# Second attention: subtraction of the maximum on GpSimd, fields paired five apart, three pairs in flight

## The reference

```
cols = _unfold(y, WS, STRIDE, PAD)            # WS 8, STRIDE 6, PAD 3
attn = jnp.einsum('blhic,blhjc->blhij', q, k) + bias[None, None]
e = jnp.exp(attn - jnp.max(attn, axis=-1, keepdims=True))
s = jnp.sum(e, axis=-1, keepdims=True)
s_img = _reverse(s, H, W)                     # overlapping windows are added up
o = jnp.einsum('blhij,blhjc->blhic', e, v)
o_img = _reverse(o, H, W).reshape(B, HEADS, ch, H, W)
out = (o_img / s_img[:, :, None]).reshape(B, C, H, W)
out = _hft(_conv1x1(out, proj_w, proj_b), hft_w, hft_b)
```

## Time and profile before

| what | us |
|---|---|
| time, median of 3 runs | 5556.05 |
| lowest, highest | 5555.84, 5556.2 |
| the profiled execution: its time | 5562.28 |
| the profiled execution: its span | 5560.1 |
| second attention in it, first DMA to last store issued | 2513.2 to 3004.6 |

### The profile page before, as it was taken

The page is one execution under the profiler, slowest core; times in us unless marked ns, Lnnn a source line. Parts: engine busy times, 40 slices in busy tenths (PEclk is TensorE's granted clock), DMA queues, the critical chain, the costliest instruction groups (busy, mean ns, idle before and its releaser), DMA issues. The chain is left out here.

```text
span 5560.1 us, 84741 instructions
## 1 busy us (share of the span) xinstructions
PE 5052.6 (91%) x33796; PEld 2334.1 (42%) x33796; DVE 3792.1 (68%) x4563; ACT 2672.0 (48%) x3851; POOL 1419.3 (26%) x1156
## 2 busy tenths in 40 slices
PE   7799999999989998997886989999896999999989
PEld 2255555555544443445553433333332333333333
DVE  3476767767651112227987849998686999999953
ACT  1134444444442222324553135554475888888854
POOL 1000000000000001112223410000002999999930
PEclk9899999999989998998998999999997999999999
DMA  6521211112113122434443410000233475447454
GB/s 217 155 39 23 44 35 29 38 24 42 23 28 118 68 71 93 134 109 139 139 135 113 144 50 20 30 30 20 87 111 124 161 177 180 170 163 177 164 180 159
DMA packets 322564, 550.69 MB, mean 99 GB/s; under 512 B 147660, under 2 KB 283492, under 8 KB 318812
## 3 DMA queue, kind: packets, MB, share of 16 engines
q1 hardware_dynamic: 295900, 465.09, 28.1%
q0 software_dynamic: 15232, 63.76, 3.5%
q10 hardware_dynamic: 11040, 16.43, 1.0%
HBM read 379.09 MB, written 166.09 MB: 98 GB/s over the span
## 5 line engine op out<-in xcount | busy, mean ns | idle before, releaser
L3926 DVE TENSOR_TENSOR_SCAN s_h<-s_da,s_h 128x448 f32<-128x448 f32 x672 | 730.2, 1128 | 26.1 <-ACT s_da L3853 22.6
L3973 POOL TENSOR_TENSOR s_h<-s_dtu,s_bt 128x896 f32<-128x896 f32 x336 | 698.7, 2080 | 0.1
L3783 PE MATMUL s_py<-s_prod,s_idf 128*128 128x448 f32 x1344 | 573.9, 549 | 0.0
L623 PE MATMUL b_pc<-b_ca,b_wdm 128*113 128x392 f32 x1152 | 487.2, 520 | 31.3 <-DVE b_wdm L838 25.5
L766 ACT ACTIVATE b_band<-b_psel 124x784 f32<-124x784 f32 x264 | 217.4, 823 | 427.5 <-PE b_psel L691 424.4
L3853 ACT ACTIVATE s_da<-s_dt,s_al 128x448 f32<-128x448 f32 x672 | 401.9, 637 | 13.0 <-DVE s_h L3926 12.9
L623 PE MATMUL b_pc<-b_cb,b_wdm 128*113 128x392 f32 x960 | 402.0, 519 | 0.0
L1268 POOL MEMSET kept_f_wt<- 128x192 f32 x1 | 0.3, 257 | 1415.9 <-POOLq L144 1415.9
L3933 DVE TENSOR_TENSOR s_prod<-s_h,s_pc 128x896 f32<-128x896 f32 x336 | 356.8, 1062 | 1.4 <-issue 0.7
L2862 DVE SCALAR_TENSOR_TENSOR j_zc<-j_zt,kept_vec,j_zc 128x896 f32<-128x896 f32 x320 | 345.0, 1146 | 6.7 <-ACT j_zt L2804 6.4
L3783 PEld LDWEIGHTS s_py<-s_prod,s_idf 128*128 128x128 f32 x1344 | 246.4, 190 | 187.7 <-issue 167.0
(11 more groups left out here) (724 smaller groups left out, 10900.3 us busy)
## 6 DMA issues: line engine op xcount, KB each, us to landing
s_bt<-mid_brs SPq DMA_DIRECT2D x112, 896.0 KB, 4.4
s_bt<-mid_brs SPq DMA_DIRECT2D x112, 448.0 KB, 5.8
b_qk<-mid_qkvp SPq DMA_DIRECT2D x96, 240.2 KB
d_vt<-mid_vd SPq DMA_DIRECT2D x200, 96.0 KB
d_qs<-mid_qd SPq DMA_DIRECT2D x20, 744.0 KB, 5.7
d_ks<-mid_kd SPq DMA_DIRECT2D x20, 744.0 KB, 7.9
b_v<-mid_qkvp SPq DMA_DIRECT2D x6, 1922.0 KB
mid_pout<-d_out POOLq DMA_DIRECT2D x20, 558.0 KB, 4.3
```

The lines of the kernel that those rows point to most:

```text
L623: mm = pe.matmul(pc[n % 2][0:113, 0:392], wdm[:, slot, p, 0:113], src, start=(w == STARTS[a]), stop=(w + 1 == STARTS[a + 1]))
L3783: mm = pe.matmul(y, idf[:, :], prod[j % 3][:, e, :], start=(pr == 0 and e == 0), stop=False)
L3926: v.tensor_tensor_scan(x, along(da[m % 3][:, 0, 0:CH]), x, before_, ALU.mult, ALU.add).then_inc(scanned, 1)
L3973: p.tensor_tensor(h[j % HR][:, :, :], u, bt[t % BR][:, 2 * pr:2 * pr + 2, :], ALU.mult).then_inc(fed, 1)
```

## The change

Four things change together in `window_strips`.

1. The subtraction of the maximum leaves VectorE. GpSimd gets `shift(n)`, one instruction a pair over 768 elements.
2. A pair is fields i and i+5 instead of 2i and 2i+1. They don't overlap, so `lay(n)` is one instruction of 768 elements.
3. Three pairs are in flight: `d_sc` and `d_mx` are triple, PE, DVE and GpSimd run two pairs ahead (score(n+2), soft(n+2), shift(n+2)) where PE and DVE ran one ahead.
4. GpSimd's other work is cut up between the subtractions: one of the three window copies of the next strip at i = 0, 1 and 2, the clearing at i = 3. The store is issued by SyncE.

```diff
-        sc = [sb(f"d_sc{i}", [128, 2, 3 * 2 * 64]) for i in range(2)]
-        mx = [sb(f"d_mx{i}", [128, 12]) for i in range(2)]
+        sc = [sb(f"d_sc{i}", [128, 2, 3 * 2 * 64]) for i in range(3)]
+        mx = [sb(f"d_mx{i}", [128, 12]) for i in range(3)]
...
                 for k in range(2):
-                    x = STEP * (2 * i + k)
+                    x = STEP * (i + NP * k)
                     sp.dma_start(vt[n % NV][64 * k:64 * k + 64, :], vd[q, STEP * r:STEP * r + WS, x:x + WS, :]).then_inc(v_loaded[n % NV], 16)
...
                 if n + NV < NW:
                     values(n + NV)
+                if s >= 2 and i == 0:
+                    store(s - 2)
...
+            def shift(n):
+
+                p.wait_ge(max_found, n + 1)
+                p.tensor_tensor(group(n), group(n), mx[n % 3][:, :].rearrange("p (m o) -> p m o", o=1).broadcast_to([128, 12, 64]), ALU.subtract).then_inc(shifted, 1)
+
+            for t in range(3):
+                window(0, t)
             clear(0)
-            for s in range(NSTR):
-                if s + 1 < NSTR:
-                    window(s + 1)
+            shift(0)
+            shift(1)
+            for n in range(NW):
+                s, i = divmod(n, NP)
+                if n + 2 < NW:
+                    shift(n + 2)
+                if i == 0 and s % NR:
+                    carry(s)
+                if s + 1 < NSTR and i < 3:
+                    window(s + 1, i)
+                if s + 1 < NSTR and i == 3:
                     clear(s + 1)
-                if s:
-                    store(s - 1)
-                if (s + 1) % NR:
-                    carry(s + 1)
...
             score(0)
+            score(1)
             for n in range(NW):
                 s, i = divmod(n, NP)
-                if n + 1 < NW:
-                    score(n + 1)
+                if n + 2 < NW:
+                    score(n + 2)
                 turn(n)
...
             def soft(n):
-                o = n % 2
                 v.wait_ge(scored, n + 1)
-                if n >= 2:
-                    v.wait_ge(turned, n - 1)
-                v.tensor_tensor(sc[o][:, :, :], pS[:, :, 0:384], bt[:, :, :], ALU.add).then_inc(biased, 1)
+                if n >= 3:
+                    v.wait_ge(turned, n - 2)
+                v.tensor_tensor(sc[n % 3][:, :, :], pS[:, :, 0:384], bt[:, :, :], ALU.add).then_inc(biased, 1)
                 v.wait_ge(biased, n + 1)
-                by = sc[o][:, :, :].rearrange("p b (m j) -> p (b m) j", j=64)
-                v.tensor_reduce(mx[o][:, :], by, AX.X, ALU.max).then_inc(max_found, 1)
-                v.wait_ge(max_found, n + 1)
-                v.tensor_tensor(by, by, mx[o][:, :].rearrange("p (m o) -> p m o", o=1).broadcast_to([128, 12, 64]), ALU.subtract).then_inc(shifted, 1)
+                v.tensor_reduce(mx[n % 3][:, :], group(n), AX.X, ALU.max).then_inc(max_found, 1)
...
-                for k in range(2):
-                    x = STEP * (2 * i + k)
-                    dst = acc[s % 2][:, :, :, x:x + WS]
-                    if 2 * n + k:
-                        v.wait_ge(laid, 2 * n + k)
-                    v.tensor_tensor(dst, dst, pO[:, k, 0:384].rearrange("p (a h w) -> p a h w", a=6, h=WS), ALU.add).then_inc(laid, 1)
+                if n:
+                    v.wait_ge(laid, n)
+                dst = pair(acc[s % 2][:, :, :, STEP * i:STEP * i + WS])
+                v.tensor_tensor(dst, dst, pO[:, :, 0:384].rearrange("p k (a h w) -> p k a h w", a=6, h=WS), ALU.add).then_inc(laid, 1)
```

More of the change, by code:

```diff
@@ L1992, in window_strips @@
         lo, hi = slice(0, 64), slice(64, 128)
+        group = lambda n: sc[n % 3][:, :, :].rearrange("p b (m j) -> p (b m) j", j=64)
         def windows(t):
@@ L1997, in windows, with pair @@
             return bass.AP(tensor=a.tensor, offset=a.offset, ap=[list(a.ap[0]), [STEP, NR], [PW, WS], [1, WS]])
+        def pair(t):
+            a = t.copy()
+            return bass.AP(tensor=a.tensor, offset=a.offset, ap=[list(a.ap[0]), [STEP * NP, 2]] + [list(x) for x in a.ap[1:]])
         @block.sync
@@ L2016, in values, with store @@
                 for k in range(2):
-                    x = STEP * (2 * i + k)
+                    x = STEP * (i + NP * k)
                     sp.dma_start(vt[n % NV][64 * k:64 * k + 64, :], vd[q, STEP * r:STEP * r + WS, x:x + WS, :]).then_inc(v_loaded[n % NV], 16)
+            def store(s):
+                q, r = divmod(s, NR)
+                sp.wait_ge(p_evac, 3 * (s + 1))
+                sp.dma_start(rows(pout)[q, :, :, ON * r:ON * r + ON], out[s % 2][:, :, :]).then_inc(stored[s % 2], 16)
             strips(0)
@@ L2033, in _, with window @@
                     values(n + NV)
+                if s >= 2 and i == 0:
+                    store(s - 2)
+            store(NSTR - 2)
+            store(NSTR - 1)
+            sp.wait_ge(stored[0], 16 * NR)
+            sp.wait_ge(stored[1], 16 * NR)
         @block.gpsimd
         def _(p):
-            def window(s):
+            def window(s, t):
                 p.wait_ge(q_loaded[s % 2], 16 * (s // 2 + 1))
@@ L2040, in window @@
                     p.wait_ge(scored, NP * (s - 1))
-                for t in range(3):
-                    p.tensor_copy(qw[s % 2][:, t, :, :].rearrange("p n (h w) -> p n h w", w=WS), windows(qs[s % 2][:, t, :])).then_inc(windowed, 1)
+                p.tensor_copy(qw[s % 2][:, t, :, :].rearrange("p n (h w) -> p n h w", w=WS), windows(qs[s % 2][:, t, :])).then_inc(windowed, 1)
             def clear(s):
@@ L2051, in carry @@
             def carry(s):
-                p.wait_ge(laid, 2 * NP * s)
+                p.wait_ge(laid, NP * s)
                 p.tensor_copy(acc[s % 2][:, :, 0:2, :], acc[(s - 1) % 2][:, :, STEP:WS, :]).then_inc(acc_ready, 1)
[L2056 to L2061, removed]
-            clear(0)
-            for s in range(NSTR):
-                if s + 1 < NSTR:
-                    window(s + 1)
-                    clear(s + 1)
-                if s:
-                    store(s - 1)
-                if (s + 1) % NR:
-                    carry(s + 1)
-            store(NSTR - 1)
-            p.wait_ge(stored[0], 16 * NR)
-            p.wait_ge(stored[1], 16 * NR)
+            def shift(n):
[3 more added lines that the diff above has]
+                window(0, t)
+            clear(0)
+            shift(0)
[9 more added lines that the diff above has]
+                if s + 1 < NSTR and i == 3:
+                    clear(s + 1)
         @block.tensor
@@ L2089, in score @@
                     for k in range(2):
-                        x, at = 2 * i + k, 128 * t + 64 * k
+                        x, at = i + NP * k, 128 * t + 64 * k
                         for g in range(4):
@@ L2102, in turn @@
                     for t in range(3):
-                        mm = pe.transpose(pT[:, b, 128 * t:128 * t + 128], sc[n % 2][:, b, 128 * t:128 * t + 128], idf[:, :])
+                        mm = pe.transpose(pT[:, b, 128 * t:128 * t + 128], sc[n % 3][:, b, 128 * t:128 * t + 128], idf[:, :])
                 mm.then_inc(turned, 1)
@@ L2110, in weigh @@
                 if n:
-                    pe.wait_ge(laid, 2 * n)
+                    pe.wait_ge(laid, n)
                 for t in range(3):
@@ L2162, in expo @@
                 a.wait_ge(shifted, n + 1)
-                a.activation(sc[n % 2][:, :, :], sc[n % 2][:, :, :], ACT.Exp).then_inc(exp_done, 1)
+                a.activation(sc[n % 3][:, :, :], sc[n % 3][:, :, :], ACT.Exp).then_inc(exp_done, 1)
             def turn(n):
@@ L2171, in invert @@
             def invert(s):
-                a.wait_ge(laid, 2 * NP * (s + 1))
+                a.wait_ge(laid, NP * (s + 1))
                 if s:
@@ L2244, in _ @@
             soft(0)
+            soft(1)
             for n in range(NW):
                 s, i = divmod(n, NP)
-                if n + 1 < NW:
-                    soft(n + 1)
+                if n + 2 < NW:
+                    soft(n + 2)
                 if n:
```

## The result

| | median, us | runs | against the kernel before |
|---|---|---|---|
| before | 5556.12 | 4 (5555.84 to 5558.31) | |
| after | 5621.73 | 4 (5617.24 to 5630.24) | 1.0119 (95% interval 1.0101 to 1.0137) |

The change costs 65.6 us. Forecast were 5618 and a range of 5576 to 5646.

The account below looks back on a forecast made before the run. VectorE was taken to bound the old kernel at 23.4 us a strip. The new round, 24.9 plus 2.1 for the clock, is 27.0; over 18 strips +65, last strip -2.7, total +62 on 5556.05: 5618 us, range 5576 to 5646.

Parts of the forecast that it names:

- What bounds before: Second attention stage, old kernel: VectorE sets the pace, busy 21.4 of 23.4 us a strip, 91%.
- Weighing to Q's issue, 1.27: SyncE: from the end of weighing a strip's last pair, two V loads go out before Q is issued, 1.27 us.
- Q's load, 6.0: From Q's issue to GpSimd's first window copy: 6.0 us mean over 18 strips, taken as load time.
- Copy, subtract, copy, subtract, copy, 5.8: GpSimd's queue once Q lands: three copies of 0.68 and two subtractions of 1.8 us, 5.8 with hand-offs.
- my lower bound of 1.6: GpSimd's subtraction of 768 elements: taken as 1.8 us from another stage's rows, bounds 1.6 and 2.1.
- that collision: GpSimd against VectorE's division, within the dearer-GpSimd rival: 3.0 us a subtraction, 29.4 a strip, 5661 us; chance 0.09.
- TensorE's three rounds, 11.8: TensorE after the copies: scores, transposes and weighing three times, both projection parts between, 11.8 us until the next Q request.
- the clock, 2.1: TensorE after its stop runs at granted clock 0.50, adding 2.1 us to every strip.
- The stop: TensorE stands still 6 us a strip before the scores of pair 5s+5, waiting for the window copies.
- The edges: First and last strips: strip 0 about even; the last, without copies, about 15.8 instead of 18.5 us, -2.7.
- The rival with Q in time: Window copies aren't late, TensorE and VectorE run at 19 us a strip: -82 us, 5474; chance 0.05.
- TensorE's stops put to issue: TensorE idle once a strip near the end of the large loads, like one of 3.31 us; claimed no extra cost.

Follow-up runs that it names:

- e7: Kernel before the change with only fields paired five apart and a single addition of 768 elements a pair: 5552.2 us, ratio 0.9988.
- e3: Changed kernel with seven extra, unread matmuls ahead of TensorE's wait for the window copies, from strip 2 on: 5595.7 us, 25.4 us a strip.
- e1: Changed kernel with SyncE asking for the Q strip one strip earlier, nothing else: 5546.9 us, 22.5 us a strip.
- e9: e8 with the Q load moved to pair 3, so not back to back with K: 5516.0 us, ratio to the kernel before 0.9925.
- e8: e1 with the three window copies together at pair 0; Q and K load back to back: 5547.2 us, 22.7 us a strip.
- e12: e8 with K in three buffers and both strips loaded in 248 KB blocks, one or two a pair, two strips ahead: 5520.4 us.

## Why the prediction was right, step by step

1. **What bounds before.** VectorE, 23.4 us a strip. Held, though by the trace it is busy 373.5 of the 421.3 us, 89% and not 91; e7 took 0.73 us a strip of VectorE's busy time away and got 0.36 back.
2. **Weighing to Q's issue, 1.27.** The same at the start of the shown strip; at its end 2778.06 - 2776.57 = 1.49. Mean of 18: 1.32.
3. **Q's load, 6.0.** Mean over the 18 strips 5.95.
4. **Copy, subtract, copy, subtract, copy, 5.8.** 6.05 (2756.39 to 2762.44), but by two errors that cancel. The subtraction takes 1.47 us, start to start 1.42, not 1.8, and lies even under my lower bound of 1.6; that gave 0.7 back. Why the line through GpSimd's rows of another stage doesn't hold here, whether for the repeated operand or for what ran beside them, was not tried. Against it, the middle copy takes 1.81 instead of 0.68: it collides with VectorE's division, which takes 2.14 (mean 1.80 over the stage, 1.37 in the earlier trace rows). I had named that collision, among the rivals, and not priced it; it costs 1.1, in nearly every strip, on a copy or on a subtraction. That the two errors nearly cancel is luck.
5. **TensorE's three rounds, 11.8, and the clock, 2.1.** 13.9 expected, 14.1 measured (2762.44 to 2776.57), 14.0 as mean. e3 splits it: at least 1.8 of it is the clock.
6. **The stop.** "It stands still for 6 us": 5.77 in the shown strip, 5.6 as mean of 18, 3.1 to 7.1.
7. **The edges.** Strip 0 about even: from first scores to first logarithm 28.8 us before and after. Last strip -2.7 expected, -2.4 measured.
8. **What it would cost if the cause were removed.** This was wrong. The rival with Q in time was put at 19 us a strip and 5474; e1 has 22.5 and 5547, and the best order 21.3. The step that failed is the sentence on TensorE's stops put to issue, "it falls into the new idle time and costs nothing more": true of the changed kernel, where TensorE lost 14 us to them, and false as soon as the idle time is gone. The floor of 17.2 us a strip left them and the clock behind them out. In the best order (e9) they are 2.0 us of a strip.

By terms, as means of the 18 strips, a strip is 1.32 + 5.95 + 6.02 + 13.96 = 27.25, against a sum of 27.0. The 3.84 us more than before, times 18, are 69; less 2.4 at the end.

The rule of the Trainium skill on plain arithmetic (GPSIMD Engine Reference, Performance versus the Vector engine), worth an estimated 1.69 us for the subtraction, came closer than my 1.8, and is still above the 1.47 measured.

By the one on the shared port pair (the Trainium skill, SBUF — State Buffer, SBUF: two separate sides), whichever of a GpSimd instruction and a VectorE one with two SBUF inputs starts first holds the pair, and the other waits until it is done. The trace agrees, but for some 0.1 us of overlap: in the shown strip the division starts at 2757.59, while the subtraction of 2757.07 runs to 2758.54, and ends 1.19 us behind that, at 2759.73; the second copy starts at 2758.49 and ends 0.57 us behind the division, at 2760.30. In rounds of e1 where the copies came earlier the division took 1.32 (at 2742.23) and the copies 0.72.

## What to carry to other kernels

Before work is moved to a queue that works in order, ask what that queue waits for: one wait for a DMA, harmless as long as nobody needed the queue, holds up all that is put behind it. When a consumer is moved a step earlier, move the load that feeds it as well; the load's own time hadn't changed here, only its slack. And a relief for the busiest engine is worth what the next one leaves: reckon the next one's stops and its clock into the floor, not its busy time alone.

## What was not expected of the hardware

- A subtraction of 768 elements on GpSimd, the second operand repeated 64 times along the innermost axis, takes 1474 ns (1467 to 1487 over 100 in e1), 1.5 times VectorE's 958. Rows of another stage scaled to 1.8 us; why they are dearer was not tried.
- Where GpSimd's instructions met VectorE's division, a window copy of 0.71 us took up to 1.90, a subtraction of 1.47 up to 2.55 and the division of 1.31 up to 2.6.
- Useless matmuls in a wait, 5.8 us a strip, saved 26 us in all.
- Two loads of 744 KB back to back go with more of TensorE's stops without a named releaser (52 us in 18 strips of e8) than the same loads some 10 us apart (36 us in e9); blocks of 248 KB didn't lower it further (37 us in e12).
- 239 of 244 of the longer stops of this kind, besides those that end with K's landing, end 1.15 to 1.65 us after a 16 KB packet of the queue called instruction.
